# Reordering the first cross-attention stage: constants and tables behind the first units, two early folds, a longer opening burst

## The reference, cut to what matters

```python
x = x + xattn0(layernorm(x), ctx, ctx, mask_keys)      # stage A: 8 heads of 4 dims, 154 keys
x = x + ffn0(layernorm(x))                             # stage B: conv, causal attention (16 heads), 4 experts
x = x + xattn1(layernorm(x), ctx, mask_x)              # stage C: 16 heads of 64 dims, 154 keys
x = x + ffn1(layernorm(x))                             # stage D: 64 small relu networks

def xattn0(Q, K, V, Wq, bq, Wk, bk, Wo, bo, mask):
    Ql, Kl = heads(Q @ Wq.T + bq), heads(K @ Wk.T + bk)
    attn = softmax(where(mask, -inf, Ql @ Kl.T / 2))
    return concat_heads(attn @ V) @ Wo.T + bo
def xattn1(x, context, mask, Wq, Wkv, Wout, bout):
    k, v = split(context @ Wkv); q = x @ Wq
    attn = softmax(heads(q) @ heads(k).T / 8 - (1 - mask) * 1e6)
    return concat_heads(attn @ heads(v)) @ Wout + bout
```

## Time and profile before

| | us |
|---|---|
| three runs | 352.04, 352.2, 356.1 |
| median | 352.2 |
| profiled execution, its own time | 353.55 |
| its span, first to last instruction | 351.7 |
| PE busy | 319.3 |
| DVE busy | 242.5 |
| ACT busy | 215.6 |
| POOL busy | 119.2 |

### The profile page before, as it was taken

How to read it: one execution, slowest core, us unless ns; L and a number is a source line. 1 busy time by engine, 2 the same in 40 slices (tenths; PEclk the granted TensorE clock), 3 DMA queues, 4 the chain that set the end, 5 groups by cost and what they waited for, 6 DMA issues and landing times.

```text
span 351.7 us, 6759 instructions
## 1 busy us (share of the span) xinstructions
PE 319.3 (91%) x2375; PEld 228.0 (65%) x2375; DVE 242.5 (69%) x608; ACT 215.6 (61%) x633; POOL 119.2 (34%) x150
## 2 busy tenths in 40 slices
PE   6876999998899898997999999999699999999696
PEld 2334887764566544434543899897488787878684
DVE  4787786486799988762640563277878967887565
ACT  1378887246135456564678654664768586676895
POOL 3415555001330033330423062410577535445300
PEclk9699999999999999999999999999999999999899
DMA  7590000037786400008202002200100000000002
GB/s 217 190 258 2 0 2 2 2 107 230 202 282 174 102 0 2 2 3 304 58 3 84 0 9 75 77 9 1 54 15 18 0 0 2 1 3 0 0 2 61
DMA packets 21590, 22.44 MB, mean 64 GB/s; under 512 B 3606, under 2 KB 18358, under 8 KB 21558
## 3 DMA queue, kind: packets, MB, share of 16 engines
q1 hardware_dynamic: 19750, 19.93, 19.2%
q0 software_dynamic: 512, 1.05, 1.0%
q10 hardware_dynamic: 1296, 1.05, 0.9%
HBM read 14.22 MB, written 7.60 MB: 62 GB/s over the span
## 4 chain that ended last, share of the span: by engine, by line
PE 59%; DVE 24%; ACT 9%; issue 5%; DMA 1%; POOL 1%; SPq 0%; ACTq 0%; POOLq 0%; DVEq 0%
PE PS L1294 50%; DVE mB L828 9%; PE PS L1342 6%; ACT big L1104 2%; ACT big L1270 2%; DVE big L666 2%; DMA big<-in_A_WkT 1%; ACT big L1222 1%; DVE big L639 1%; DVE mraw L631 1%; DVE mraw L655 1%; DVE U L622 1%; ACT big L1078 1%; DVE XN L622 1%; PE PS L1309 1%
## 5 line engine op out<-in xcount | busy, mean ns | idle before, releaser
L1294 PE MATMUL PS<-big 128*128 128x128 f32 (+10 forms) x592 | 95.7, 313 | 9.2 <-DVE big L639 3.3
L1294 PEld LDWEIGHTS PS<-big 128*128 128x128 f32 (+3 forms) x592 | 58.1, 152 | 43.2 <-issue 15.4
L510 POOL TENSOR_TENSOR big<-big,urec 128x1024 f32<-128x1024 f32 x24 | 45.6, 1898 | 65.2 <-DVE urec L673 45.5
L1104 ACT ACTIVATE big<-big 128x154 f32<-128x154 f32 x192 | 60.4, 319 | 7.3 <-DVE big L666 4.9
L1222 ACT ACTIVATE big<-PS 128x1024 f32<-128x1024 f32 (+3 forms) x64 | 42.1, 703 | 24.6 <-PE PS L1294 23.7
L828 DVE TENSOR_REDUCE mB<-PS 128x2 f32<-128x256 f32 (+5 forms) x90 | 50.1, 622 | 6.9 <-PE PS L1294 6.8
L1078 ACT ACTIVATE big<-PS 128x1280 f32<-128x1280 f32 (+2 forms) x30 | 32.6, 1092 | 33.9 <-PE PS L1342 30.9
L1294 PE MATMUL PS<-cstb 128*128 128x128 bf16 x192 | 37.9, 220 | 0.0
L1294 PE MATMUL PS<-kkC,XT 128*128 128x462 f32 (+1 forms) x96 | 36.0, 510 | 1.6 <-DVE big L666 1.6
L498 POOL TENSOR_TENSOR rstd<-ve,minus_half 128x4 f32<-128x4 f32 (+2 forms) x13 | 13.2, 1016 | 70.8 <-DVE ve L617 70.8
L1342 PE MATMUL PS<-cst,big 128*128 128x128 f32 x240 | 31.1, 278 | 5.9 <-ACT big L1078 3.0
(11 more groups left out here) (187 smaller groups left out, 481.3 us busy)
## 6 DMA issues: line engine op xcount, KB each, us to landing
scr_qk<-big SPq DMA_DIRECT2D x12, 384.0 KB, 3.8
big<-scr_qk SPq DMA_DIRECT2D x16, 288.0 KB
big<-in_wv SPq DMA_DIRECT2D x1, 2048.0 KB, 8.2
scr_x<-zrow SPq DMA_DIRECT2D x2, 448.0 KB, 6.4
scr_y<-big SPq DMA_DIRECT2D x2, 448.0 KB, 3.0
X<-in_x ACTq DMA_DIRECT2D x2, 256.0 KB, 3.6
big<-in_A_WoT ACTq DMA_DIRECT2D x1, 512.0 KB, 4.4
cw<-in_C_Wk SPq DMA_DIRECT2D x1, 512.0 KB, 5.1
```

The lines of the kernel that those rows point to most:

```text
L510: pool.tensor_tensor(pn[:, 0:GH * P].rearrange("p (h k) -> p h k", h=GH), Pt[u % 3][:, :, 0:KM], r.to_broadcast([P, GH, KM]), ALU.mult).th ...
L1104: i = act.activation(Pt[u % 3][:, h, :], Pt[u % 3][:, h, :], ACT.Exp, accum_out=usum[:, u % 3, h:h + 1])
L1294: return pe.matmul(o, lhsT, rhs, start=start, stop=stop)
```

## The change

- DVE's `constants` run after round 3 instead of after round 0.
- POOL's tables, from zrow on, wait for both shifts of unit 0. The memset of woutZ stays where it was.
- The loads of three of stage C's weights count on a semaphore of their own (`ld_k`), so that the first two folds need neither woutZ nor the end of stage A. `F_START = 2`: fold 0 stands in round 2 of PE in place of the eight `hold_clock` matmuls, fold 1 at the end of that round, both in bank 7; ACT copies them after its rounds 1 and 2. The groups of three at rounds 8, 9 and 10 are now folds 2 to 4, 5 to 7 and 8 to 10.
- One fold of stage A (eight matmuls of 32x128) moves ahead of unit 1's scores, and ACT's copies around it are reordered.
- The opening burst has 15 matmuls instead of 11.

```diff
-        F_UNIT = (3, 6, 9)
+        F_START = 2
+        F_UNIT = (5, 8, 11)
...
         def fold_bank(n):
+            if n < F_START:
+                return 7
...
-            sp.dma_start(wkC, i["C_Wk"]).then_inc(ld_c, 16)
-            sp.dma_start(wvC, i["C_Wv"]).then_inc(ld_c, 16)
-            sp.dma_start(wqT, i["C_WqT"].rearrange("(c p) d -> p c d", p=P)).then_inc(ld_c, 16)
+            sp.dma_start(wkC, i["C_Wk"]).then_inc(ld_k, 16)
+            sp.dma_start(wvC, i["C_Wv"]).then_inc(ld_k, 16)
+            sp.dma_start(wqT, i["C_WqT"].rearrange("(c p) d -> p c d", p=P)).then_inc(ld_k, 16)
...
             pool.memset(woutZ, 0.0).then_inc(zeroed, 1)
+            pool.wait_ge(unit_shift["A"], 2)
             pool.memset(zrow[:], 0.0).then_inc(zeroed, 1)
...
-            units_A({0: constants, NT - 1: lambda: ln_u_stats(0), NT: lambda: ln_b_stats(0)})
+            units_A({3: constants, NT - 1: lambda: ln_u_stats(0), NT: lambda: ln_b_stats(0)})
...
             def first_copies():
+                copy_A(2, 3)
                 queries_A(1)
-                copy_A(2, 4)
-
-            units("A", {0: first_copies, 1: lambda: copy_A(4, len(PREA)),
-                        NT: lambda: copy_C(0, F_UNIT[0]),
+                copy_A(3, len(PREA))
+
+            units("A", {0: first_copies, 1: lambda: copy_C(0, 1), 2: lambda: copy_C(1, F_START),
+                        NT: lambda: copy_C(F_START, F_UNIT[0]),
...
                 elif st == "A":
                     pe.wait_ge(q4_ready, B)
+                    pe.wait_ge(preC_act, sum(j[2] for j in PREC[:F_START]))
...
                     if u == 2:
                         pe.wait_ge(q4_ready, B)
-                        hold_clock(OUT_BANK["A"], 8)
+                        fold_C(0, 1)
...
                     if n == 0:
-                        pe.wait_ge(ld_c, 80)
+                        pe.wait_ge(ld_k, 48)
+                    elif n < F_START:
+                        pe.wait_ge(preC_act, done[n])
+                    elif n == F_START:
+                        pe.wait_ge(ld_c, 32)
                         pe.wait_ge(unit_shift["A"], SHIFTS["A"] * NT)
...
-            hold_clock(6, 11)
+            hold_clock(6, 15)
...
             def first_gap():
                 fold_A(0, 2)
                 turn("a", XN, (1,))
+                fold_A(2, 3)
 
             def folds_A():
                 queries_A(1)
-                fold_A(2, len(PREA))
+                fold_A(3, len(PREA))
...
-            units_A({0: first_gap, 1: folds_A, NT: lambda: fold_C(0, F_UNIT[0]),
+            units_A({0: first_gap, 1: folds_A, 2: lambda: fold_C(1, F_START), NT: lambda: fold_C(F_START, F_UNIT[0]),
```

More of the change, by code:

```diff
@@ L288, in program @@
         zeroed = sem("zeroed")
+        ld_k = sem("ld_k")
         onesb_ready = sem("onesb_ready")
```

## The result

| | executions | median, us | over the kernel before |
|---|---|---|---|
| kernel before | 22 | 354.37 | |
| changed kernel | 22 | 357.04 | 1.0079, 95% interval 1.0054 to 1.0103 |

The change made the kernel **slower, by 2.8 us (1.9 to 3.6)**. The forecast was 352.0 us against a median of 352.2, so no change, with a range of 349.7 to 354.4, so the measured 0.8% more lies outside it. The three executions that the forecast started from were also on the low side: over 22 executions the kernel before has a median of 354.37 us, not 352.2. The profiled execution of the changed kernel took 355.55 us, its span is 353.5 us.

The account below looks back on a forecast made before the run. DVE and PE passing units back and forth bound stage A, then a chain through PE alone. -0.6 + 0.45, rounded to -0.2 us, on 353.55 profiled, with the median 1.35 lower, gave 352.0 us; range 349.7 to 354.4.

Parts of the forecast that it names:

- The opening: Start of stage A: four more burst matmuls keep PE's clock high, first maximum at 12.75 instead of 15.05, 2.3 us won.
- Rival C: Opening: the clock falls all the same and the moved constants cost more than their old place; 354.0 us, chance 0.2.
- POOL's tables: Unit 0 of stage A: with tables behind the shifts, its clamp waits 0.4 us instead of 0.78; unit 1's waits 0.1.
- Constants leave round 0: DVE, round 0 of stage A: 2.34 us from reciprocal to next maximum shrink to a steady round's 1.15, 1.2 us won.
- constants in round 3: DVE beside POOL's norm, each blocking the other: unit 4 starts at 33.8, 0.6 us earlier than before; bounds 0.3 to 1.5.
- Early folds: PE, rounds 2 and 3 of stage A: 0.3 us delay ahead of unit 3's scores, bounds 0 and 1; unit 3 at 26.2.
- Groups of three: PE between the last two weighings: the folds take 2.0 instead of 1.58 us, 0.45 us lost.
- Two folds fewer there give nothing, because DVE covers them.: Later folds of stage C, beside DVE's rotations and layer norms: no gain; 1.05 us if DVE were not the longer.
- a moving later stage: Sign of being wrong: a later stage, held unchanged in the forecast, moves by more than the end does.
- the good side of the line: PE's idle gaps: 1.96 us came before no clock fall, 2.15 and 2.25 did; the opening's shorter gap should keep it.
- The sum: Whole kernel: -0.6 us at unit 4 plus 0.45 for the last folds, -0.15, rounded to -0.2 us.

Follow-up runs that it names:

- b_hold15: The kernel before with 15 instead of 11 matmuls in the opening burst and nothing else: 353.6 us, ratio 0.9996 to the kernel before.
- a_hold11: The changed kernel with 11 opening matmuls as before: 356.81 us, ratio 1.0098 to the kernel before.
- ctrl_after2: The changed kernel run again without any edit, second repeat: 356.49 us, ratio 1.0077 to the kernel before.
- b_const3: The kernel before with only the constants moved behind round 3: 357.09 us, ratio 1.0088 to the kernel before.
- ctrl_after: The changed kernel run again without any edit, first repeat: 356.64 us, ratio 1.0105 to the kernel before.
- best: The changed kernel without early folds, half of X added in round 0, other constants behind layer norm b's application: 351.54 us, ratio 0.9933 to the kernel before.
- a_foldback: The changed kernel without its two early folds, the eight idle matmuls back in round 2: 354.17 us, ratio 1.0022 to the kernel before.
- a_foldback2: Second sample of the changed kernel without its two early folds: 353.99 us, ratio 1.0027 to the kernel before.
- a_fill: The changed kernel with 8 idle matmuls filling PE's gap at 81 us: 355.45 us, ratio 1.006 to the kernel before.
- ctrl_before: The kernel before, unchanged, run against itself as a control: 355.42 us, ratio 1.0042.

## Why the prediction was wrong, by its own steps

**The opening: first maximum at 12.75, "2.3 us won". This is the step that failed.** Its mechanism was right in the profile, and its place too: no idle PE behind the burst, queries in 1.10 us, first maximum at 13.09. The fault was to count it in full in the sum. Over the executions it is worth 0.1 us (`b_hold15`; by its interval between 1.3 gained and 1.0 lost) and 0.3 us (`a_hold11` beside `ctrl_after2`). I compared one profiled execution with itself, less its one visible fall, while the number of falls varies from execution to execution: the kernel before had mean clocks from 0.971 to 0.995 in one group of executions. Rival C had the size (354.0) but not the mechanism: the clock did hold. One reading on the way was off and did no harm: a slice from 8.8 us that is low for 0.8 of it would end at 15.8 us, not at 14.9; the short stretches have the clock back between 14.5 and 15.

**POOL's tables, 0.4 us.** The clamp of unit 0 took 0.25 instead of 0.95 us, that of unit 1 0.17. Right in the trace, and better than reckoned, since the memset of woutZ ended just behind the maximum, at 14.78. No run tests the tables alone.

**Constants leave round 0, 1.2 us; constants in round 3.** Forecast 33.8 for unit 4, measured 33.47. The pair of additions ended at 32.33, forecast 32.65, so the hold-up is real and both ways. The Trainium skill (SBUF, State Buffer, "Who interferes with whom") says that a DVE instruction with two inputs in SBUF and a GpSimd instruction that reads SBUF block each other for the whole instruction; the 2.94 and 2.23 us agree. Right in the trace: 3.04 - 1.2 = 1.9 us net, where the prediction had 3.3 - 1.2 = 2.1. In time `b_const3` puts it at 3.1 us (2.1 to 4.2), so the waits don't account for all of it. What the prediction left out is that the hold-up leaves PE idle too: 1.97 us ahead of 38.35 in `b_const3`, 2.71 us ahead of 37.02 in `ctrl_after2`, each with a fall behind it, and 2.70 us ahead of 36.47 in `ctrl_after` without one. Between 26 and 44 us the kernel before and `best` have no idle PE over 1.7 us.

**Early folds, bounds 0 and 1 us.** Unit 3 at 26.17; right. **Groups of three, 0.45 us.** From 63.27 to 65.18 are 1.91 us instead of 1.58, so 0.33; right.

**"Two folds fewer there give nothing, because DVE covers them." This is a second step that failed.** They did give nothing to the sum of waits, as it says. But the prediction held the later stages unchanged, and by `a_foldback` and `a_foldback2` the early folds cost 2.5 us in the changed kernel where it had 0.3 + 0.45. It had named a moving later stage as what would prove it wrong. They left PE idle for 1.8 us; that this idle time is the cause is not shown (`a_fill` gives 1.2 us, not clear of the control), and the eight idle matmuls lost in round 2 may have their part. A gap of 1.81 us is below the 1.96 us that I had called the good side of the line, and there is no such line in these runs: behind gaps of 1.80 and 1.81 us a fall came in three profiles and none in four, and behind the 1.55 us ahead of 118 us one came after the change and none before it.

**The sum, mended.** With 0 for the opening in place of -2.3 it is -0.2 + 2.3 = +2.1 us, within the 1.9 to 3.6 measured (2.8; 3.7 and 2.7 in the two repeats). What makes up the rest is not settled, since the parts don't add: -0.4 for the tables, 3.1 for the constants by `b_const3` and 2.5 for the early folds by the two runs without them would be 5.2, far over 2.8.

**Falls over all executions.** Fitted over 316 executions here, with a level for each kernel, 0.0048 less mean clock (one fall of 3.4 us in 354) goes with 1.0 us more, and with 1.2 when the one execution at 0.936 is left out; `ctrl_before` was expected to show 1.5. The changed kernel has 0.981, the one before 0.987 over its four groups: 1.2 falls more, which by this fit go with 1.2 to 1.4 of the 2.8 us, although the two of the opening are gone. The Trainium skill (TensorE: Matmul & The Clock Gate, "What's actually happening") says that the monitor behind the clock is free-running, so where it stands at a program's start varies. The profiles fit this, without showing the cause: the kernel before had its fall behind the opening at 332 us once and at 160.5 and 335 us another time, the changed one at 30, 84, 118 and 334, at 116, 161 and 335, and at 36, 118, 163 and 337 us. The prediction knew this rule and used it for rival C alone; it bears on every term that is a fall.

**What stays open.** How much of what a high opening wins is paid back by falls in stage A and how much otherwise; why taking back the early folds gives 2.5 us beside constants in round 3 and at most about 1 us without them; and what sets the number of falls of a kernel: gaps of 0.9 to 2.7 us stood ahead of the falls in these profiles, and the same gaps stood elsewhere without one. A filler in the long wait of round 3 was not tried.

## What to carry to other kernels

A term that consists in the clock's falling or not falling is not worth what one profile shows: look at the mean clock over many executions, and test it by itself. Don't hold later stages unchanged without a reason when work moves out of them, even where another engine covers it: here taking two such folds back gave 2.5 us. And put constants on DVE where it waits for another engine and POOL is idle: the same instructions took 4.1 us beside a norm (29.39 to 33.47), 3.4 beside memsets (16.34 to 19.72) and 2.3 alone, and in `best` nobody waited for them.

## What the runs showed that I had not expected

- The clock fell behind gaps of only 1.5 to 1.8 us in an otherwise busy TensorE (81.4, 116.3 us in the changed kernel), and in other executions didn't behind the same gaps.
- The same fall of 3.4 us cost stage A nothing inside the long wait of round 3 and 1.4 us right behind it (54.5 and 56.1 beside 54.7 us).
- Idle matmuls that left no fall at their place in the profiles taken (7.5, 114 us) brought no time over all executions; at a third place (83 us) they may have brought 1.2 us, within what the control allows.
- One program, run again beside itself, differed by 0.4% with an interval of 0.1 to 0.8%.
